# Second half of a two-layer mixer: slot weights by way of DRAM, roots on GpSimd

## What is computed

```
# layer 0
xn = layernorm(x);  Q = xn @ Wq + bq;  s = softmax(Q Q^T / sqrt(128)) @ Q
logits = xn @ phi_w^T + phi_b              # 64 experts x 32 slots = 2048 columns
D = softmax(logits over the slots of an expert);  C = softmax(logits over the experts)
X~ = D^T xn (over all tokens); X~ = tanh(layernorm(clip(X~)));  Y~ = X~ @ expert_w + expert_b
x  = x + s * silu(C @ Y~)
# layer 1
xn = layernorm(x);  i, r = sigmoid(gates(xn));  a = exp(8 r log(sigmoid(lam)))
h_t = a_t h_(t-1) + sqrt(1 - a^2 + 1e-6) * (i * x_proj);   s = rmsnorm(h) @ W_out
g = sigmoid(xr @ W_r) * (relu(xk @ W_k)^2 @ W_v)    # xr, xk: xn mixed with the token before
x = x + s * silu(g)
```

## Time and profile before

| | |
|---|---|
| median of 3 runs | 1347.46 us (1346.07 to 1348.26) |
| profiled execution | 1348.3 us, of it 1346.2 us span from the first to the last instruction |
| TensorE busy | 1252.0 us (93%) |
| DVE busy | 1051.1 us (78%) |
| ScalarE busy | 740.2 us (55%) |
| GpSimd busy | 814.2 us (60%) |
| mean granted TensorE clock | 0.98 of full speed |

### The profile page before, as it was taken

How to read it: one execution, slowest core, us unless ns; L and a number is a source line. 1 busy time by engine, 2 the same in 40 slices (tenths; PEclk the granted TensorE clock), 3 DMA queues, 4 the chain that set the end, 5 groups by cost and what they waited for, 6 DMA issues and landing times.

```text
span 1346.2 us, 17623 instructions
## 1 busy us (share of the span) xinstructions
PE 1252.0 (93%) x4866; PEld 740.7 (55%) x4866; DVE 1051.1 (78%) x1533; ACT 740.2 (55%) x1459; POOL 814.2 (60%) x768
## 2 busy tenths in 40 slices
PE   6699999999999999998699999999999999999984
PEld 2465555555555555553465555665555565555641
DVE  6899999999999999996455777666776667776653
ACT  2655556556665555653434555555655555655554
POOL 3588989999898898996244454343453344453320
PEclk9899999999999999999799999999999999999997
DMA  6433333333333333333643333333333333333310
GB/s 199 120 139 124 141 128 137 140 125 140 134 131 141 124 140 131 134 141 141 196 133 118 102 125 117 111 125 110 118 123 105 125 118 110 117 110 125 125 32 16
DMA packets 123217, 167.35 MB, mean 124 GB/s; under 512 B 7153, under 2 KB 99313, under 8 KB 122993
## 3 DMA queue, kind: packets, MB, share of 16 engines
q1 hardware_dynamic: 122688, 164.65, 35.5%
q10 hardware_dynamic: 434, 1.59, 0.4%
HBM read 90.71 MB, written 75.50 MB: 123 GB/s over the span
## 4 chain that ended last, share of the span: by engine, by line
PE 37%; POOL 5%; DVE 4%; issue 4%; ACT 0%; POOLq 0%; DVEq 0%
PE yac L797 12%; PE ct L785 6%; POOL b_e L1331 5%; PE at L854 4%; PE at L844 2%; DVE nmx L1180 2%; PE lp L894 1%; PE lp L906 1%; PE lp L900 1%; DVE b_ti L1259 1%; PE lp L139 1%; PE lp L869 1%; PE at L830 1%; PE at L833 1%; PE at L832 1%
## 5 line engine op out<-in xcount | busy, mean ns | idle before, releaser
L562 POOL TENSOR_TENSOR dd<-ed,rz 128x512 f32<-128x512 f32 x256 | 263.4, 1050 | 58.9 <-DVE rz L551 58.9
L463 PE MATMUL acc<-dd,xns 128*128 128x512 f32 x512 | 260.9, 592 | 1.3 <-POOL dd L562 1.3
L797 PE MATMUL yac<-cf,expert_out 128*128 128x512 f32 x512 | 261.7, 594 | 0.0
L1167 DVE TENSOR_TENSOR cf<-ct,slot_weight 128x512 f32<-128x512 f32 x256 | 175.3, 685 | 87.1 <-PE ct L785 84.1
L498 ACT ACTIVATE ed<-lg 128x512 f32<-128x512 f32 x256 | 138.9, 595 | 84.7 <-PE lg L448 84.7
L538 DVE TENSOR_REDUCE mr<-lg 128x32 fp32r<-128x1024 f32 x128 | 154.6, 1208 | 26.0 <-PE lg L434 26.0
L785 PEld LDWEIGHTS ct<-identity,exp_slots_loaded 128*128 128x128 f32 x1024 | 127.7, 142 | 80.1 <-issue 67.3
L570 POOL TENSOR_TENSOR slot_weight<-exp_slots_loaded 128x512 f32<-128x512 f32 x128 | 164.5, 1286 | 0.0
L432 PE MATMUL lg<-phi_transposed,xn_transposed 128*128 128x512 f32 x256 | 158.4, 619 | 2.2 <-PEq L359 1.8
L504 ACT ACTIVATE exp_slots_loaded<-lg 128x512 f32<-128x512 f32 x256 | 139.0, 595 | 30.3 <-PE lg L454 30.2
L546 DVE TENSOR_REDUCE zd<-ed 128x32 f32<-128x1024 f32 x128 | 154.8, 1209 | 1.0 <-ACT ed L498 1.0
(11 more groups left out here) (187 smaller groups left out, 2242.0 us busy)
## 6 DMA issues: line engine op xcount, KB each, us to landing
exp_slots<-exp_slots_loaded SPq DMA_DIRECT2D x128, 512.0 KB, 2.7
exp_slots_loaded<-exp_slots SPq DMA_DIRECT2D x128, 512.0 KB, 3.4
xns<-xn_rows SPq DMA_DIRECT2D x128, 64.0 KB, 1.7
expert_w<-in_expert_w SPq DMA_DIRECT2D x8, 512.0 KB, 5.3
b_xraw<-in_xT SPq DMA_DIRECT2D x16, 256.0 KB, 3.7
out_t<-b_ti SPq DMA_DIRECT2D x16, 256.0 KB, 4.1
xn_rows<-slot_max SPq DMA_DIRECT2D x2, 1024.0 KB, 5.1
xn_rows<-slot_sum SPq DMA_DIRECT2D x2, 1024.0 KB, 5.3
```

What stands on the lines that cost most here:

```text
L463: e.matmul(acc[k][:, :], xns[w % RX][:, :], dd[w % RX][:, bank(k)], start=tile == 0, stop=tile == NT - 1, skip_group_check=True).then_inc( ...
L562: e.tensor_tensor(dd[v % RX][:, bank(k)].rearrange("q (n p) -> q n p", p=NP), ed[c][:, bank(k)].rearrange("q (n p) -> q n p", p=NP), rz[c] ...
L797: e.matmul(yac[:, :], YF[:, c, :], cf[c % RC][:, :], start=c == 0, stop=c == CH - 1).then_inc(c_y)
L1167: e.tensor_tensor(cf[c % RC][:, :], ct[c % 2][:, :], WT[i % 2][c // (CH // HALVES)][:, :], ALU.mult).then_inc(c_w)
```

## The change

The diff has these parts.

- **Statistics by way of DRAM.** `slot_max` and `slot_sum` no longer live through the second half. They are stored to DRAM in the second block (the last 16 tiles of the second expert half in the middle block), and `join_load` brings those of one batch back, in `slot_max_batch` and `slot_sum_batch`, one batch ahead (for batch 0 in the middle block, behind the experts' weights and biases in SP's queue).
- **Slot weights turned in two passes and spread by transfers.** `join_weights` writes 32 columns once for each half and tile, so that one 128x128 transpose turns the four tiles of a half. ScalarE copies the two transposed tiles, `join_stored` writes them to DRAM, and `join_spread` reads them back in eight transfers, which put them on four groups of 32 partitions. `weighted` waits for these at c = 0. The join runs earlier in the iteration: `join_inverse` at c = 4 instead of 7, `join_sums` at 3 instead of 5, `join_weights` at 5 instead of 8, the turn at 5 instead of 11, the copy at 6 instead of 11.
- **Centring matrix.** `mean` multiplies with identity minus 1/128, so that the centred tile stands in PSUM; `centre` goes, and `squares` and `normalise` read PSUM.
- **Roots as GpSimd powers.** The three pairs of logarithm and exponential go. Two become a copy with an added epsilon on ScalarE and `tensor_tensor` with `ALU.pow` and a broadcast column of -0.5 on GpSimd (`inverse_deviation`, `inverse_state_norm`); `input_scale` is such a power with 0.5, at c = 0 instead of 4. The table loads in the loop go as well. The square of the decay moves from ScalarE to DVE.
- **Fewer copies and other places.** `yt` goes: `silu_y` reads `yac` itself, and the next batch's `combine` waits for `silu_y`. `keep` goes, with two buffers for the residual instead. `qh` is written by ScalarE straight from PSUM, `xh` by a ScalarE copy (`normalised_high`), and the four `weighted_rows` move from GpSimd to ScalarE (c = 5, 6, 7, 7).

The core of the diff:

```diff
+        def join_load(e, b):
             if b:
                 e.wait_ge(s_wp, WP * b)
-            e.tensor_tensor(MJ[:, :, :], joined(SM, b)[:, 0], joined(SM, b)[:, 1], ALU.max).then_inc(s_wv)
+            for k, dst in ((0, MS), (1, ZS)):
+                e.dma_start(dst[:, :, :, :], STATS[:, k, :, b * TPB:(b + 1) * TPB, :]).then_inc(s_st, 16)
+
+        def join_max(e, b):
+            e.wait_ge(s_st, 32 * (b + 1))
+            e.tensor_tensor(MJ[:, :, :], MS[:, 0], MS[:, 1], ALU.max).then_inc(s_wv)
...
+            e.tensor_tensor(WR[:, :, :, :], MS[:, :, :, :], both_halves(MJ[:, :, :]), ALU.mult).then_inc(s_wp)
+
+        def join_turned(e, b, out):
+            e.wait_ge(s_wp, WP * (b + 1))
             for h in range(HALVES):
...
+                done = e.transpose(out[:, h * TILE:(h + 1) * TILE], WR[:, h, :, :].rearrange("q t p -> q (t p)"), IDENT[:, :])
             done.then_inc(s_wt)
...
+        def join_stored(e, b):
+            e.wait_ge(s_wc, b + 1)
+            if b >= 2:
+                e.wait_ge(s_wl, 16 * WL * (b - 1))
+            e.dma_start(WD[b % 2].rearrange("h r k -> r h k"), WS[:, :, :]).then_inc(s_wd, 16)
+
+        def join_spread(e, b):
+            e.wait_ge(s_wd, 16 * (b + 1))
+            for j in range(EPC):
+                for h in range(HALVES):
+                    e.dma_start(WT[b % 2][j * NP:(j + 1) * NP, h, :].rearrange("p (t k) -> p t k", t=TPB),
+                                WD[b % 2][h].rearrange("(t p) k -> p t k", p=NP)).then_inc(s_wl, 16)
```

```diff
             def sync1b(e):
...
+                e.wait_ge(s_stat, 64)
+                join_load(e, 0)
+                for k, src in ((0, SM), (1, SS)):
+                    e.dma_start(STATS[:, k, 1, EARLY:NT, :], src[:, 1, EARLY:NT, :]).then_inc(s_stat, 16)
...
                 for g in range(RL):
                     load_exps(e, g)
+                join_stored(e, 0)
+                join_spread(e, 0)
+                join_load(e, 1)
                 for g in range(RW, GROUPS):
...
             def sync2(e):
...
+                        if k == 3 and i + 1 < NB:
+                            join_stored(e, i + 1)
+                        if k == 4 and i + 1 < NB:
+                            if i:
+                                e.wait_ge(c_w, i * CH)
+                            join_spread(e, i + 1)
                         if k == 5:
                             store(i - 2)
+                            if i + 2 < NB:
+                                join_load(e, i + 2)
```

```diff
                     if c == 0 and i:
-                        e.wait_ge(y_c, i)
+                        e.wait_ge(S["u_y"], i)
...
-                        e.matmul(lp[0][:, :], MEAN[:, :], B["x1"][:, :], start=True, stop=True).then_inc(S["mn"])
+                        e.matmul(lp[0][:, :], CENTRE[:, :], B[f"x1{i % 2}"][:, :], start=True, stop=True).then_inc(S["mn"])
...
+                def weighted_rows(i, r):
+                    if within(i):
+                        E = B[f"e{r}"][:, :]
+                        e.wait_ge(A["z"], i * TPB + r + 1)
+                        e.activation(E, E, ACT.Identity, scale=one(nmx, 4 * r + 3)).then_inc(A["p"])
...
+                def variance_copied(i):
+                    if within(i):
+                        e.wait_ge(S["vr"], i + 1)
+                        e.activation(B["ty"][:, :], lp[1][:, :], ACT.Identity, bias=one(EPS, 0)).then_inc(S["vc"])
...
                         if c == 2:
                             value_high(i)
-                        if c == 4:
-                            input_scale(i - 2)
+                            if i + 1 < NB:
+                                join_factors(e, i + 1)
+                        if c == 5:
+                            weighted_rows(i, 0)
+                        if c == 6:
+                            weighted_rows(i, 1)
+                            if i + 1 < NB:
+                                join_copied(e, i + 1, lp[1])
                         if c == 7:
+                            weighted_rows(i, 2)
+                            weighted_rows(i, 3)
                             squares(i - 1)
                         if c == 8:
-                            state_norm(i - 2)
+                            state_mean_copied(i - 2)
                         if c == 9:
                             turn_high(i, 0)
-                            deviation(i - 1)
+                            variance_copied(i - 1)
+                        if c == 10:
+                            normalised_high(i - 1)
...
+                def inverse_deviation(i):
+                    if within(i):
+                        e.wait_ge(S["vc"], i + 1)
+                        e.tensor_tensor(B["ty"][:, :], B["ty"][:, :], one(EPS, 5).broadcast_to([P, SEQ]), ALU.pow).then_inc(S["rs"])
...
+                        if c == 0:
+                            input_scale(i - 2)
+                        if c == 8:
+                            inverse_state_norm(i - 2)
+                        if c == 9:
+                            inverse_deviation(i - 1)
```

More of the change, by code:

```diff
@@ L40, in build @@
     RE = 4
+    EARLY = 48
     GC = 2
@@ L84, in build @@
         EC = nc.dram_tensor("exp_slots", (HALVES, NT, TILE, HS), F32).ap()
[L86 to L88 removed]
+        STATS = nc.dram_tensor("slot_statistics", (P, 2, HALVES, NT, NP), F32).ap()
+        WD = [nc.dram_tensor(f"slot_weights{b}", (HALVES, TPB * NP, TILE), F32).ap() for b in range(2)]
+        s_xnd = sem("xn_stored")
+        s_in = sems("rows_then_experts_loaded", 4)
+        s_exp = sems("exp_slots_stored_then_loaded", RE)
+        STORED = 16 * UNITS // RE
+        ROWS = 16
+        s_stat = sem("statistics_stored")
+        s_st = sem("join_statistics_loaded")
         s_wp = sem("join_gpsimd")
@@ L415, in sync1 @@
                     if v == 0:
-                        for k in range(4):
-                            e.wait_ge(s_xnd[k], 16)
+                        e.wait_ge(s_xnd, 64)
                     if v >= RX:
@@ L594, in build @@
             py = [psum(ph, f"py{k}", [P, BANK]) for k in range(2)]
-            pw = [psum(ph, f"pw{k}", [P, SEQ]) for k in range(HALVES)]
+            pw = psum(ph, "pw", [P, SEQ])
             s_eb = sem("pb_expert_b")
-            s_ew = sems("pb_expert_w", RW)
             s_cl = sem("pb_clipped")
@@ L666, in scalar1b @@
                     e.activation(XTT[:, bank(q)], xc[:, bank(q)], ACT.Tanh).then_inc(s_th)
-                for h in range(HALVES):
-                    join_copied(e, 0, h, pw[h])
             def vector1b(e):
@@ L710, in build @@
             LAG = 3
-            RC = 4
             SCALE = float(P) ** -0.5
-            cf = [sb(ph, f"cf{k}", [P, SEQ]) for k in range(RC)]
-            yt = sb(ph, "yt", [P, SEQ])
-            names = ("qf", "e0", "e1", "e2", "e3", "st", "xraw", "ty", "x1", "xc", "x1k",
+            RF = 4
+            cf = [sb(ph, f"cf{k}", [P, SEQ]) for k in range(RF)]
+            names = ("qf", "e0", "e1", "e2", "e3", "st", "xraw", "ty", "x10", "x11",
                      "vf", "ti", "tg", "aa", "a2", "hh", "xr", "xk", "kr", "f1")
@@ L727, in build @@
             x_prev = XP[:, 0:SEQ]
-            c_t, c_w, c_y, y_c = (sem("c_" + n) for n in ("turned", "weighted", "y", "y_copied"))
+            c_t, c_w, c_y = (sem("c_" + n) for n in ("turned", "weighted", "y"))
             s_zero = sem("zero_column")
@@ L978, in query @@
                         e.activation(B["qf"][:, :], at[0][:, :], ACT.Identity, bias=one(VEC, V_BQ)).then_inc(S["q_f"])
+                        if i:
+                            e.wait_ge(A["s"], i * TPB)
+                        e.activation(R["qh"][:, :], at[0][:, :], ACT.Identity, bias=one(VEC, V_BQ)).then_inc(S["q_h"])
                 def value_high(i):
@@ L1085, in ffn_tanh @@
                         e.activation(B["xr"][:, :], B["kr"][:, :], ACT.Tanh, scale=0.25).then_inc(S["tf"])
-                def input_scale(i):
-                    if within(i):
-                        e.wait_ge(S["om"], i + 1)
-                        e.activation(B["a2"][:, :], B["a2"][:, :], ACT.Ln, bias=one(EPS, 1)).then_inc(S["sl"])
-                        e.wait_ge(S["sl"], i + 1)
-                        e.activation(B["a2"][:, :], B["a2"][:, :], ACT.Exp, scale=0.5).then_inc(S["sr"])
                 def state_squares(i):
@@ L1145, in scalar2 @@
                             state_squares(i - 2)
-                        if c == 9 and within(i - 1):
-                            e.preload_act_table_set("exp_and_others")
-                        if c == 11:
-                            if i + 1 < NB:
-                                for h in range(HALVES):
-                                    join_copied(e, i + 1, h, lp[h])
                         if c == 12:
@@ L1289, in vector2 @@
                             weights(i, 0)
+                            if i + 1 < NB:
+                                join_inverse(e, i + 1)
                         if c == 6:
```

(4 more changed lines are left out.)

262 lines of the change are left out of this document (112 added, 150 removed), and 4 rows, old and new, of the table S.

## The result

The changed kernel takes 5176.53 us (median of 4 runs, 5175.59 to 5178.24) where the kernel before takes 1347.86 us (4 runs, 1346.07 to 1350.05): the ratio is 3.84, 95% interval 3.834 to 3.847. The forecast was 1413 us with a range up to 1525, with slower at 0.78. The direction came true; the time lies 3,650 us above the top of the range.

What follows compares the result with a forecast made beforehand. TensorE was taken to set the second half's pace. Batches +51, batch 1 +1.5, batch 0 transposes -0.65, middle stage +9.5, tail +4.7 made +66 us on 1348.3, or 1413 us in the median; range 1340 to 1525.

Steps and rivals of the forecast that it cites:

- P: Time of one root as a GpSimd power on a 128x512 tile, taken as 3.5 us.
- The likeliest case: Roots on GpSimd with P from 2 to 4.5 us: 1377 to 1448 us, chance 0.33.
- the rival called spine: Roots on GpSimd set the pace, P from 4.5 to 6.1 us: 1448 to 1501 us, chance 0.25.
- The formula: Start of `weigh(1)`: a batch lengthens by max(0, P - 0.5, 2P - 3.3), 3.6 us at P = 3.5, +51 over 14 batches.
- The period would be unchanged with free roots: At `weigh(1)`: later `variance`, about 0.87 us, balances the 0.87 us of transposes gone at c = 11.
- New wait 1: The gate: next batch's first product (c = 3) waits for DVE's `silu_y`, 1.3 us lost.
- new wait 2: The join: TensorE waits 1.07 us to turn the slot weights, now at c = 5 instead of 11.
- this lateness swallows the wait at `state_mean`: TensorE, late from the join, reaches `state_mean` at 955.4, after the squares at 955.1, so no wait there.
- The removed waits: TensorE's old waits at `state_mean` (0.77 us) and the attention rows' first turn (0.63 us) go.
- The ordinary root: A root is an ordinary GpSimd operation, P near 1.04 us: 1362 us, between 1350 and 1375, chance 0.22.
- Faster: TensorE regains waits at `state_mean` and `turn(0)` if P is below 1.3 and new waits under 2 us: 1325 us, chance 0.20.
- that rival: The clock: TensorE waits of 3.6 us a batch lower its granted clock, +24 us: 1437 us; no separate chance given.

Runs made afterwards that it cites:

- the 1374.67: Changed kernel with the three roots back on ScalarE as logarithm and exponential and the table loads restored: 1374.67 us, ratio 1.019 to the kernel before.
- the best version: Changed kernel with ScalarE roots, `yt` restored, slot-weight turn moved, batch 0's statistics read from SBUF, its spreads issued later: 1319.28 us, ratio 0.978.

## Why the prediction was wrong

**The step that failed: the price of a root.** The prediction took P = 3.5 us and gave 6.1 as the upper bound, from the reciprocal's row on DVE, "nearer in kind, since a power is no single arithmetic step". P is 81.9. Both numbers carried a ratio from one engine to another. The reciprocal of 128x512 on DVE was measured behind the powers: 3.35 us, 5 times a plain operation, so the analogy described DVE rightly; on GpSimd a power is 80 times a product. The estimate from the Trainium skill (GPSIMD Engine Reference, "Performance versus the Vector engine", 12 cycles for branching) was 5.1 us, 16 times too low; no run here bears it out for a power. The likeliest case, both ends of its range and the rival called spine all stood on the same analogy, so the range had no end that could hold the price.

**What hung on P was right in shape.** The formula said that a batch gets longer by 2P - 3.3 and that the third root is free up to P = 7.2. At 81.9 that is 160.5 + 74.7 = 235.2 us; the trace has 279.9 - 40.8 = 239.1. (At P = 3.5 the formula gives 3.7 us, where the sum took 3.6.) The places were nearly as foreseen: the wait in `weigh` (line 904), and the third root holding `query_low`. The prediction had TensorE wait for the first two roots together, in `weigh`; in fact the slot products behind `output` stop it for the length of the first one at line 835.

**"The period would be unchanged with free roots" was wrong.** With the roots on ScalarE, where they were, it is 1.2 us longer. New wait 1 was right (1.3 foreseen, 1.2 measured), and new wait 2 nearly so (1.07 against 0.84 in the mean and 1.1 at the longest). What failed is "this lateness swallows the wait at `state_mean`": it looked only at the squares, and missed that `state_mean` now also waits for the copy of the turned weights out of its PSUM tile, 14.4 us in 520. The removed waits went as said. The rival with a root of 1.04 us, nearly free, gave 1362 us, 13 under the 1374.67; this wait, 1.1 us each of 13 times, is of that size.

**The row scalings were under-sized.** The prediction counted 0.63 us for the wait at the turn. Moved alone they bring 24 us, as the wait at `state_mean` ends with them, by way of GpSimd's order and of DVE's two slowed operations.

**The middle block was right.** 9.5 us foreseen, 9.2 measured; the first part, the late maximum, was put at 7.5 us and is 648.11 - 639.94 = 8.2 with the roots on ScalarE and 6.3 in the changed kernel itself, where it starts at 646.25. No wait of TensorE in the steady state is for a spread or a trip by way of DRAM: the best version has them all and keeps TensorE busy for 477.4 of 480 us.

**Rivals.** The ordinary root falls by the measured price, and so do the spine's figures (1448 to 1501), though its mechanism is what happened. Faster failed twice: by the price, and with the roots taken out, by the new waits: the two foreseen come to 14.6/12 + 10.1/12 = 2.1 us a batch, already at its limit of 2, and the third makes it 3.2. Its gain was read rightly all the same: it counted 2.05 us a batch, and with the new waits repaired a batch gains 2.1. The clock fell as that rival said, to 0.57 where TensorE waits. TensorE's lines are only 6% of the chain now, and its busy time grew by 121 us, some 8 a batch; how much of this lies in the 34 us beside the roots was not separated.

## What to carry to other kernels

Before a function moves to an engine on which no row of the trace shows it, run it once by itself, at two widths: one of one column (0.54 us here) would have shown nothing. An unknown price is not bounded by a ratio seen on another engine, and a range built on one analogy should say so. When a step is moved, list every semaphore that its PSUM or SBUF tile now brings with it, at its own place and at the places of those that share the tile; and where TensorE waits less than a microsecond a batch behind a chain, look at what runs on GpSimd beside each DVE operation of that chain.

## What the runs showed of the hardware

- GpSimd's power costs 0.16 us a column: 81.9, 41.1 and 20.7 us for 512, 256 and 128 columns of 128 partitions, 81.9 for 32 partitions, and the same for a tile of ones and for exponents of -0.5, 0.5 and 2. A product of 128x512 beside them took 1.03 us. Powers on DVE were not tried.
- DVE's operations with two tiles in SBUF take 0.69 us at 128x512, but 0.94 to 1.64 us in the mean where they ran beside GpSimd's operations with two tiles in SBUF (`b_ti` of line 1259 beside the join's sums, and `b_ti` of line 1277, which began at 959.59 us beside the products of line 133 and takes 0.69 with the row scalings on ScalarE). GpSimd's side is slowed as well: the sum of line 122 takes 0.78 us beside `b_x` and 0.47 alone. The slot products, with one input in PSUM, stay at 0.68. The row scalings, with one tile and a column, do no such harm: `b_x` at 943.07 ran beside one in 0.69 us. The Trainium skill says the same of the Vector instruction's inputs (GPSIMD Engine Reference, "Key points": contention with Vector instructions that have two SBUF inputs); how much it costs stands in the rows above.
- Small loads did not overtake: two loads of 128 KB, queued behind four of 512 KB and four of 256 KB, kept DVE idle for 8.9 us, and put first they gave back 7.7 us.
